# A second level of Strassen's scheme for product 1 of the W_base stage, over couples of pairs

## The reference

```python
def _L0_cond_ref(v, q, W3, b3, W2, b2):
    q_emb = jax.nn.relu(q @ W3 + b3)
    v_sum = jnp.sum(v, axis=1, keepdims=True)
    x = (n * v + v_sum) * q_emb[:, None, :]
    return jax.nn.relu(x @ W2 + b2)

def _L0_ffn_ref(x, W_base, b_base, A_s, B_s, A_r, B_r, W_router, b_router):
    base_out = einsum('bsd,df->bsf', x, W_base) + b_base
    shared_out = (x @ A_s) @ B_s
    gates = softmax(x @ W_router + b_router)
    ...
    return base_out + shared_out + routed_out   # top 2 of 6 experts, rank 16 each

x = x + _L0_ffn_ref(_L0_cond_ref(x, cond_1024, ...), ...)
```

## Time and profile before

| | us |
|---|---|
| median of 3 runs (1410.85 to 1411.5) | 1411.26 |
| span of the profiled execution | 1409.3 |
| TensorE busy in it | 1405.1 |
| DVE busy | 909.1 |
| ACT busy | 607.0 |
| POOL busy | 18.8 |

### The profile page before, as it was taken

The page is one execution under the profiler, slowest core; times in us unless marked ns, Lnnn a source line. Parts: engine busy times, 40 slices in busy tenths (PEclk is TensorE's granted clock), DMA queues, the critical chain, the costliest instruction groups (busy, mean ns, idle before and its releaser), DMA issues.

```text
span 1409.3 us, 18037 instructions
## 1 busy us (share of the span) xinstructions
PE 1405.1 (100%) x6177; PEld 1156.1 (82%) x6177; DVE 909.1 (65%) x1563; ACT 607.0 (43%) x1140; POOL 18.8 (1%) x65
## 2 busy tenths in 40 slices
PE   9999999999999999999999999999999999999999
PEld 6888888888888888888888888888888888888887
DVE  6977565765656656567889566655655656556564
ACT  7774645546455464645544231332312323132230
POOL 3000000000000000000000000000000000000000
PEclk9999999999999999999999999999999999999999
DMA  8242414334142342426727527163361634617242
GB/s 315 81 159 84 158 50 141 104 91 154 55 140 98 104 148 59 144 82 223 267 92 210 190 95 249 63 219 137 110 241 61 232 119 136 216 60 268 84 148 91
DMA packets 135580, 200.03 MB, mean 142 GB/s; under 512 B 38752, under 2 KB 39008, under 8 KB 135488
## 3 DMA queue, kind: packets, MB, share of 16 engines
q1 hardware_dynamic: 134624, 197.66, 42.2%
q10 hardware_dynamic: 864, 1.22, 0.2%
HBM read 127.12 MB, written 71.70 MB: 141 GB/s over the span
## 4 chain that ended last, share of the span: by engine, by line
PE 100%; DVE 0%; DVEq 0%; issue 0%
PE ps L1633 33%; PE ps L1635 33%; PE ps L1634 33%; PE ps L1644 1%; PE ps L1659 0%; PE ps L1653 0%; DVE buf L1626 0%; DVEq L57 0%; DVE zeros L1261 0%
## 5 line engine op out<-in xcount | busy, mean ns | idle before, releaser
L1633 PE MATMUL ps<-act_hi,w_hi 128*128 128x512 f32 x1792 | 697.3, 389 | 0.0
L1635 PE MATMUL ps<-act_hi,w_lo 128*128 128x512 f32 x1792 | 697.1, 389 | 0.0
L1634 PE MATMUL ps<-act_lo,w_hi 128*128 128x512 f32 x1792 | 697.1, 389 | 0.0
L1633 PEld LDWEIGHTS ps<-act_hi,w_hi 128*128 128x128 f32 x1792 | 336.3, 188 | 70.6 <-DVE act_lo L1099 0.9
L1635 PEld LDWEIGHTS ps<-act_hi,w_lo 128*128 128x128 f32 x1792 | 336.3, 188 | 69.9
L1634 PEld LDWEIGHTS ps<-act_lo,w_hi 128*128 128x128 f32 x1792 | 336.3, 188 | 69.8
L675 ACT ACTIVATE act_hi<-src 128x512 fp32r<-128x512 f32 x256 | 156.3, 625 | 256.3 <-PE ps L1635 254.6
L1163 DVE SCALAR_TENSOR_TENSOR buf<-ps,bb_sb,buf 128x512 f32<-128x512 f32 x127 | 95.0, 750 | 157.8 <-PE ps L1635 142.1
L1106 DVE TENSOR_TENSOR act_lo<-src,act_hi 128x512 fp32r<-128x512 f32 x192 | 130.3, 684 | 36.2 <-ACT act_hi L675 36.2
L1099 DVE SCALAR_TENSOR_TENSOR act_lo<-src,shift,act_hi 128x512 fp32r<-128x512 f32 x128 | 95.2, 748 | 30.4 <-ACT act_hi L672 30.4
L694 ACT ACTIVATE yhi<-buf 128x512 fp32r<-128x512 f32 x128 | 80.0, 625 | 65.2 <-PE ps L1635 65.1
(11 more groups left out here) (119 smaller groups left out, 1018.1 us busy)
## 6 DMA issues: line engine op xcount, KB each, us to landing
src<-in_xT SPq DMA_DIRECT2D x224, 256.0 KB, 2.8
y_scratch<-buf SPq DMA_DIRECT2D x128, 256.0 KB, 2.1
src<-y_scratch SPq DMA_DIRECT2D x128, 256.0 KB, 5.1
outT<-buf SPq DMA_DIRECT2D x127, 256.0 KB, 3.8
buf<-in_xT SPq DMA_DIRECT2D x32, 256.0 KB, 5.0
wl_raw<-in_wbase SPq DMA_DIRECT2D x6, 1024.0 KB, 6.0
r<-in_w SPq DMA_DIRECT2D x15, 256.0 KB, 9.7
grow<-gates_scratch SPq DMA_DIRECT2D x96, 32.0 KB, 2.1
```

The source lines that it names most:

```text
L1633: nc.tensor.matmul(out, wh, a_h, start=start, stop=False, skip_group_check=onto)
L1634: nc.tensor.matmul(out, wh, a_l, start=False, stop=False, skip_group_check=onto)
L1635: return nc.tensor.matmul(out, wl, a_h, start=False, stop=stop, skip_group_check=onto)
```

## The change

Product 1 of pairs 2 to 7 is no longer done pair by pair. The pairs make three couples (2 and 3, 4 and 5, 6 and 7; `QUADS` holds the program index of the even one, e counts the couples). The product of the 512 x 512 weights Q12 with both pairs' G21 activations (512 features x 1024 tokens) is done as a second step of the same scheme: 7 inner products of 256 x 256 weights with 256 features x 512 tokens, each 2 output tiles x 2 contraction tiles x 3 = 12 matmuls. They stand in the even pair: one behind each group of product 0 and each of the first three groups of product 2. The partner's results wait in SBUF (`partner`) until the odd pair, which has no product 1: there DVE adds product 0's bank, the bias and the partner's tile in one instruction (`c11_partner`) in place of ACT's copy and the add.

For that, in this order:

- In pair 1 (g = 9) SP loads Q12 once more; DVE makes four sums of its quarters, ACT and DVE split the 7 inner weight sets, and POOL stores them to `inner_dram`, 512 KB each, through two staging buffers.
- In a couple POOL loads each inner set into one of two buffers (`inner_w`); a load waits for the inner product two before. POOL also loads the partner's G21 from `y_dram` into `partner` (two loads of 512 KB) and, since the inner sums overwrite G21 of the even pair, loads that again (two of 512 KB, `g21_reload`) before `t4`.
- ACT and DVE make the inner operands, two tiles (128 x 1024) an instruction: `a1_max`, `inner_high`, `inner_low`, `inner_t1` to `inner_t4`; the results are taken from banks 4, 5 and 7, 6 by `add_p0`, `add_p1`, `add_u2`, `add_u4`, `add_p6` (DVE) and `copy_v`, `copy_partner` (ACT).
- In even pairs `low_rank_c11` moves behind the groups of product 3, and `c11_add_low` into DVE's loop of product 4, `lr_low_b` into the same loop.
- Semaphores of the weights' preparation are merged to make room for the new ones; nothing of their order changes.

The core of the diff (the semaphores' arithmetic and repeated helpers are left out):

```diff
+    inner_dram = nc.dram_tensor("inner_scratch", (L2, P, 2, 2, T // 2), F32R, kind="Internal").ap()
...
+        partner = sb("partner", [P, H, T], F32, early)
+        sb("inner_pad1", [P, (NPROD - 1) * H, T], F32, early)
+        inner_w = sb("inner_w", [P, 2, 2, 2, T // 2], F32R, early)
...
+        staged_w = sb("staged_w", [P, 2, 2, 2, T // 2], F32R, early)
...
+        QUADS = tuple(range(NP + 2, ALL, 2))
+        def joined(g):
+            return g >= QUADS[0]
...
         def slot(g, n, k):
-            return H * ((g + n) % 2) + k
+            s = START[g]
+            if not joined(g):
+                return H * ((s + n) % 2) + k
+            if g % 2 == 0:
+                half = 1 - s if n in (3, 5) else s
+                return H * half + ((k + 2) % H if n == 3 else k)
+            return H * (s if n in (0, 3, 5) else 1 - s) + k
+        def inner_slot(e, m):
+            return H * (1 - START[QUADS[e]]) + 2 * (m % 2)
+        def seq(g, n):
+            return SEQ[g, n]
...
+        iq11, iq12 = inner_raw[:, 0:2, low_cols], inner_raw[:, 2:4, low_cols]
+        iq21, iq22 = inner_raw[:, 0:2, high_cols], inner_raw[:, 2:4, high_cols]
+        INNER_SETS = ((iq11, 0), (iq12, 1), (iq22, 5), (iq22, 4), (iq21, 3), (iq11, 2), (iq12, 6))
...
+                if g == QUADS[0] - 1:
+                    sp.wait_ge(bank_done, group_no(g, 1, H - 1))
+                    load_quadrant(wl_raw[:, 1], Q12, wl_loaded[1])
...
+            for k in range(L2):
+                pool.wait_ge(inner_w_lo, k + 1)
+                pool.dma_start(inner_dram[INNER_SETS[k][1]], staged_w[:, k % 2]).then_inc(inner_w_stored[k % 2], 16)
+            def inner_weights(e, m):
+                c = L2 * e + m
+                if c >= 2:
+                    pool.wait_ge(inner_done, 2 * (c - 1))
+                else:
+                    pool.wait_ge(inner_w_stored[0], 16 * 4)
+                    pool.wait_ge(inner_w_stored[1], 16 * 3)
+                pool.dma_start(inner_w[:, c % 2], inner_dram[m]).then_inc(inner_w_loaded[c % 2], 16)
+            def load_partner(e):
+                p = QUADS[e] - NP + 1
+                for h in range(2):
+                    if e > 0:
+                        pool.wait_ge(c11_done, four(QUADS[e] - 1, 2 * h + 1))
+                    for k in (2 * h, 2 * h + 1):
+                        pool.wait_ge(buf2_stored[k], 16 * (p + 1))
+                    pool.dma_start(partner[:, 2 * h:2 * h + 2, :],
+                                   y_dram[2 * p, H + 2 * h:H + 2 * h + 2].rearrange("k p t -> p k t")
+                                   ).then_inc(partner_loaded[h], 16)
+            def g21_reload(e, h):
+                pool.wait_ge(inner_lo_done, L2 * e + (4 if h == 0 else 6))
+                pool.dma_start(src[:, tile(G21, 2 * h):tile(G21, 2 * h) + 2, :],
+                               y_dram[2 * (QUADS[e] - NP), H + 2 * h:H + 2 * h + 2].rearrange("k p t -> p k t")
+                               ).then_inc(g21_again[h], 16)
+            for e in range(len(QUADS)):
+                inner_weights(e, 0)
+                inner_weights(e, 1)
+                load_partner(e)
+                inner_weights(e, 2)
+                inner_weights(e, 3)
+                inner_weights(e, 4)
+                g21_reload(e, 0)
+                inner_weights(e, 5)
+                inner_weights(e, 6)
+                g21_reload(e, 1)
...
+                even = g in QUADS
+                if even and n == 3:
+                    act.wait_ge(inner_done, inner_no(QUADS.index(g), 5 + k // 2, 1))
+                    return
+                if even and n == 5:
+                    act.wait_ge(bank_done, group_no(g, 3, H - 1))
+                    return
+                back = 1 if even and n == 2 else 2
                 if k < H - 1:
-                    act.wait_ge(op_used, used_no(g, n, k) - 2 * (H - 1))
-                else:
-                    act.wait_ge(bank_done, group_no(g, n, H - 1) - 2 * H)
+                    act.wait_ge(op_used, used_no(g, n, k) - back * (H - 1))
+                else:
+                    act.wait_ge(bank_done, group_no(g, n, H - 1) - back * H)
...
+            def inner_weight_high(k):
+                act.wait_ge(wl_loaded[1], 32)
+                if k >= 3:
+                    act.wait_ge(inner_w_sum, k - 2)
+                if k >= 2:
+                    act.wait_ge(inner_w_stored[k % 2], 16 * (k // 2))
+                nc.scalar.activation(staged_w[:, k % 2, 0], INNER_SETS[k][0], ACT.Copy).then_inc(inner_w_hi, 1)
...
+            def even(e):
+                g = QUADS[e]
+                p = g - NP
+                a1_max(e)
+                inner_high(e, 0)
+                inner_high(e, 1)
+                copy_p0(g, 0)
+                inner_high(e, 2)
+                copy_p0(g, 1)
+                inner_high(e, 3)
+                copy_p0(g, 2)
+                inner_high(e, 4)
+                for j in range(H):
+                    high(g, 2, j)
+                copy_p0(g, 3)
+                inner_high(e, 5)
+                copy_v(e, 0)
+                copy_v(e, 1)
+                lr_high_a(p)
+                inner_high(e, 6)
+                copy_u2(g, 0)
+                copy_u2(g, 1)
+                high(g, 3, 0)
+                high(g, 3, 1)
+                copy_u2(g, 2)
+                copy_partner(e, 0)
+                copy_partner(e, 1)
+                high(g, 3, 2)
+                high(g, 3, 3)
+                copy_u2(g, 3)
...
+            def c11_partner(p, j):
+                e = QUADS.index(NP + p - 1)
+                dve.wait_ge(bank_done, group_no(NP + p, 0, j))
+                dve.wait_ge(buf1_stored[j], 16 * 2 * (NP + p))
+                if j < 2:
+                    dve.wait_ge(inner_copied, copied_no(e, COPY_P4, j))
+                else:
+                    dve.wait_ge(inner_added, added_no(e, EV_U4, j - 2))
+                nc.vector.scalar_tensor_tensor(buf1[:, j, :], ps[:, j, :], bb_sb[:, j:j + 1], partner[:, j, :],
+                                               ALU.add, ALU.add).then_inc(c11_done, 1)
...
+            def inner_t1(e):
+                dve.wait_ge(a1_relu, e + 1)
+                dve.wait_ge(partner_loaded[0], 16 * (e + 1))
+                nc.vector.scalar_tensor_tensor(b1, b1, 0.0, a1, ALU.max, ALU.subtract).then_inc(inner_made, 1)
+            def inner_t2(e):
+                dve.wait_ge(inner_made, made_no(e, I1))
+                dve.wait_ge(partner_loaded[1], 16 * (e + 1))
+                for k in range(2):
+                    dve.wait_ge(buf2_stored[k], 16 * QUADS[e])
+                nc.vector.scalar_tensor_tensor(t2_half, b2_half, 0.0, b1, ALU.max, ALU.subtract).then_inc(inner_made, 1)
+            def inner_t3(e):
+                dve.wait_ge(inner_made, made_no(e, I2))
+                dve.wait_ge(inner_hi_done, L2 * e + 1)
+                nc.vector.tensor_tensor(a1, t2_half, a1, ALU.subtract).then_inc(inner_made, 1)
+            def inner_t4(e):
+                dve.wait_ge(inner_made, made_no(e, I2))
+                dve.wait_ge(inner_hi_done, L2 * e + 3)
+                nc.vector.scalar_tensor_tensor(a2, a2, 0.0, t2_half, ALU.max, ALU.subtract).then_inc(inner_made, 1)
...
+            def even(e):
+                g = QUADS[e]
+                p = g - NP
+                inner_low(e, 0)
+                inner_t1(e)
+                inner_low(e, 1)
+                inner_t2(e)
+                add_p0(e, 0)
+                add_p0(e, 1)
+                inner_low(e, 2)
+                inner_t3(e)
+                for j in range(H):
+                    t2(g, j)
+                add_p1(e, 0)
+                add_p1(e, 1)
+                inner_low(e, 3)
+                inner_low(e, 4)
+                for j in range(H):
+                    low(g, 2, j)
+                add_u2(e, 0)
+                add_u2(e, 1)
+                inner_t4(e)
+                inner_low(e, 5)
+                lr_low_a(p)
+                inner_low(e, 6)
+                add_u4(e, 0)
+                add_u4(e, 1)
+                for j in range(H):
+                    t3(g, j)
+                add_p6(e, 0)
+                low(g, 3, 0)
+                add_p6(e, 1)
+                low(g, 3, 1)
+                t4(g, 0)
+                t4(g, 1)
+                low(g, 3, 2)
+                low(g, 3, 3)
+                t4(g, 2)
+                t4(g, 3)
...
+            def odd(p):
+                g = NP + p
+                for j in range(H):
+                    t2(g, j)
+                    if j > 0:
+                        low(g, 2, j - 1)
+                    c11_partner(p, j)
+                low(g, 2, H - 1)
+                lr_low_a(p)
+                for j in range(H):
+                    low(g, 3, j)
+                    t3(g, j)
+                    t4(g, j)
+                    if j > 0:
+                        c11_add_low(p, j - 1)
+                c11_add_low(p, H - 1)
...
+            def inner(e, m):
```

(99 more changed lines are left out.)

283 lines of the change are left out of this document (228 added, 55 removed).

## The result

The changed kernel takes 1404.01 us (median of 4 runs, 1402.78 to 1404.65) against 1411.38 us for the kernel before (4 runs, 1410.85 to 1411.98). The ratio is 0.9949, 95% interval 0.9935 to 0.9962: 0.5% faster. The forecast was 1403.1 with a range of 1402.5 to 1408.4. The profiled execution spans 1401.7 us (1401.1 was forecast).

A forecast was written before the change was run, and what follows sets the result against it. The prediction took TensorE, busy 1405.1 of 1409.3 us, as the bound. Its one nonzero term, 36 matmuls x 0.2267 = 8.16 us saved, took the median 1411.26 to 1403.1 us, range 1402.5 to 1408.4.

The forecast's parts named there:

- The bound and the pace: Whole kernel: TensorE is the bound, so time is the number of matmuls times their pace, 0.2267 us each.
- The sum's only term: W_base stage: three couples save 36 matmuls x 0.2267 us on TensorE, 8.16 us; work added elsewhere costs nothing.
- Slacks in the even pair: Even pair: DVE's operands come in time; thinnest slacks 0.6 us at inner product 0, 0.4 at product 4's low-rank part.
- The odd pair: Odd pair, product 2: last low ends at U+12.5, wanted at 12.92, slack 0.4 us; lr_low_a has 0.5.
- Busy time: Even pair: DVE +14.7 us, to 66 of 95.2, ACT +8.3; odd pair: DVE loses 2.8; none on the path.
- What is late next: Even pair: c11 stored about 2.4 us later, x's return to buf1 at about T+63.5, product 5 wants it at 68.0; fits.
- The inner weights: Couples, POOL's queue: 512 KB loads land in 3.6 to 5 us, where 7.7 us are there.
- Rival 3: Couples: inner weights landing after 7.7 us delay TensorE; gain gone at 8.6, 1423.8 us at a landing of 10; 8%.
- Pair 1, the mis-sized term: Pair 1, once: weight preparation, stores and loads land by T-1.5, costing nothing; 2 to 4 us if as slow as 1 MB loads.
- The clock: Behind a TensorE wait for inner weights or DVE's lows: a granted clock fall would lose more than any rival case.
- rival 1: Couples: DVE holds up POOL's descriptors, load 3 is 1.5 us late three times, 4.6 in all, 1407.7 us; 8%.
- a few missed slacks: Four thin places in couples: operands late, TensorE waits 1 to 5 us in all, 1404.1 to 1408.3 us; 17%.

## Why the prediction was right, point by point

- **The bound and the pace.** Right: 6141 matmuls, starts still 0.2267 us apart, the inner ones too. The sum's only term was 8.16 us; 8.2 were measured in the stage, and 2.8 for one couple, where the sum has 2.72.
- **Slacks in the even pair.** The rows, DVE in pair 2 of the changed kernel; T is 884.37:

```profile
884.64 0.75 DVE L1419 SCALAR_TENSOR_TENSOR buf<-ps,bb_sb,buf 128x512 f32<-128x512 f32 x1 [2.05 <-PE ps L2066]
885.31 1.22 DVE L1851 TENSOR_TENSOR act_lo<-src,act_hi 128x1024 fp32r<-128x1024 f32 x1
886.44 1.22 DVE L1823 SCALAR_TENSOR_TENSOR partner<-partner,src 128x1024 f32<-128x1024 f32 x1
...
940.36 0.69 DVE L1781 TENSOR_TENSOR hb_lo<-hb_raw,hb_hi 128x512 fp32r<-128x512 f32 x1
```

  Inner low 0 ends at T+2.16 (2.15 forecast), hb_lo at T+56.7 (56.7). The estimated step of 1.13 for a 1024-wide op is 885.31 to 886.44. That such a timetable could be written from rows of 512-wide ops is the reason why slacks of 0.2 to 0.4 us could be relied on; the runs with one and two ops more show that they were no larger.
- **The odd pair.** U is 979.57. The last low starts at 991.32 and ends at U+12.4 (12.5 forecast).
- **Busy time.** DVE 65.0 us in the even pair (66 forecast), 48.3 in the odd one (48.4). ACT's 8.3 us are there: 30.7 us in the even pair, 6.2 more than in a pair before, and 2.1 ahead of T, since `a1_max` and inner high 0 run in the pair before.
- **What is late next.** buf1's first add waited 1.44 us for x, at T+63.6 (63.5 forecast), and it fitted.
- **The inner weights.** 3.8 us in the median, 5.5 at most; I took 3.6 to 5, and the estimate from the formula was 3.2. Rival 3 needed 8.6.
- **Pair 1, the mis-sized term.** I put 4.5 us on a store and 14 us on the last store and the four loads behind it. The stores took 6.8 in the median. In the changed kernel (count, KB, median us to landing):

```profile
inner_scratch<-staged_w POOLq DMA_DIRECT2D x7, 512.0 KB, 6.8
...
partner<-y_scratch POOLq DMA_DIRECT2D x6, 512.0 KB, 4.2
```

  The last store went out at 871.15, T-13.2 and not T-15.5, and the loads only at 878.83; the partner loads of this couple went out from 879.87 on and landed in 6.3 and 7.5 us. So partner 0 was there at about T+1.8, not at T-3.5, just when T1 wanted it. In the second execution of the same kernel T1 did wait:

```profile
886.74 1.23 DVE L1823 SCALAR_TENSOR_TENSOR partner<-partner,src 128x1024 f32<-128x1024 f32 x1 [0.61 <-DMA partner<-y_scratch]
```

  TensorE didn't wait for it, since I1 had 3.8 us more. So the conclusion ("nothing") held, but the margin of 3.6 us in front of T+2.1 did not: most of it was used up. The other price that I gave, 2 to 4 us if they land as slowly as 1 MB loads did (5.0 to 8.8), was too high: they did land like that, and it cost nothing.
- **The clock.** I wrote that a fall of the clock behind such a wait would cost more than any rival. No such wait came in this kernel; in the experiments a fall cost some 1.6 us (last section), less than rival 1's 4.6 or a few missed slacks.
- **Launch and start, the remainder.** The sum went from median to median with 1.96 us kept around the span, and put nothing on what lies ahead of the stage. The stage gave 8.2, the medians 7.4 and 7.7; with one couple the stage gave 2.8 and the medians 2.3. The executions shown reach the stage anywhere from 734.1 to 734.9, which is as much as the remainder of 0.5 to 0.8 us. That it has the same sign three times isn't explained: the merged semaphores act ahead of the stage too, and no run here separates them from scatter. The first result, 1404.01, lies 0.9 above the forecast by it, at the edge of the band that I gave 60% (1402.6 to 1404.1).

## What to carry to other kernels

With one engine at 100% and no waits, count its instructions and multiply by the distance of their starts; then spend the effort on a timetable of the engine that feeds it, op by op in its queue's order, with the step from one start to the next and not the durations. A chain of load, split and use that recurs must have other work of the bound engine beside it, as much as the chain is long: 8.0 us here (8.16 less 0.2 for the weight load), of which 4.4 were used (0.6 to send for the load, 3.8 to land). When such a schedule is finished, the number to look at isn't the feeding engine's share of the span but its smallest slack, here 0.23 us, less than half of one op.

## What the runs showed of the hardware that I had not expected

The granted clock can fall behind waits of TensorE of about 2 us. In the kernel with three more copies a load, TensorE waited 1.52 us before the start at 917.22 and 2.07 us before that at 924.97, and then, by stretches of 2 us (columns as in the earlier trace rows, the clock is the third number from the end):

```profile
922.00:924.00 2.00, 0.90 (x4) 0.40 (x3) 2.00 (x4) 0.60 (x1) 0.00 (x0) 1.00 0.99 329
924.00:926.00 2.00, 1.03 (x4) 0.87 (x5) 0.04 (x1) 0.00 (x0) 0.00 (x0) 0.91 0.96 353
926.00:928.00 2.00, 2.00 (x7) 1.51 (x6) 0.00 (x0) 0.60 (x1) 0.00 (x0) 0.50 0.21 78
928.00:930.00 2.00, 2.00 (x8) 1.63 (x7) 0.00 (x0) 0.41 (x1) 0.00 (x0) 0.73 0.01 4
```

0.50 is the 1.2 GHz level. The matmuls' starts stood 0.426 us apart instead of 0.227 for some eight of them, 1.6 us lost on top of the wait. With the inner products in a row it fell likewise in the second and third couple, but not in the first, whose two waits were as long. The second of the two waits in the first couple and in the second, then the clock over the whole first stretch and over 2 us in the second couple:

```profile
907.33 0.50 PE L2064 MATMUL ps<-act_hi,inner_w 128*128 128x512 f32 x1 [2.22 <-DVE act_lo L1851]
1087.03 0.50 PE L2064 MATMUL ps<-act_hi,inner_w 128*128 128x512 f32 x1 [2.08 <-DVE act_lo L1851]
```

```profile
884.40:925.00 40.60, 36.80 (x162) 29.86 (x161) 21.69 (x26) 11.83 (x17) 3.52 (x7) 1.00 0.37 116
1088.00:1090.00 2.00, 2.00 (x6) 1.53 (x6) 2.00 (x5) 0.67 (x2) 0.11 (x1) 0.50 0.71 219
```

The waits ahead of these two were 1.57 us (up to 902.14) and 1.68 us (up to 1081.94). With the late loads, 15 waits of 1.4 to 1.8 us, the clock stayed at 1.00. So a wait of 2 us on TensorE can cost nearly 4, but need not. What decides it isn't shown by these runs.
